# K's bias added on VectorE, the next sequence's transposes moved ahead, and a rearranged opening in a fused attention and mixing kernel

## The reference, cut to what matters

```python
h = layernorm(x) * (1 + ca) + sa
Q, K, V = h @ Wq + bq, h @ Wk + bk, h @ Wv + bv      # 16 heads of 8 channels
Q, K = elu(Q) + 1, elu(K) + 1
KV = einsum('nshd,nshm->nhmd', K, V);  Z = 1 / (einsum('nlhd,nhd->nlh', Q, K.sum(1)) + 1e-6)
h1 = layer_norm(h + (Q @ KV * Z) @ Wo + bo)          # g1, beta1
a  = layer_norm(h1 + relu(h1 @ W1 + b1) @ W2 + b2)   # g2, beta2
x  = x + ga * a
h2 = layernorm(x) * (1 + cb) + sb
x  = x + gb * sigmoid(mix_r(h2) @ W_r) * (relu(mix_k(h2) @ W_k)**2 @ W_v)
```

## Time and profile before

| what | value |
|---|---|
| median of 3 runs | 162.54 us (162.42 to 162.72) |
| the profiled execution, its own time | 162.81 us |
| its span in the trace | 160.7 us |
| PE busy | 155.6 us, 97% of the span |
| PEld busy | 145.1 us, 90% |
| VectorE busy | 123.1 us, 77% |
| ScalarE busy | 127.3 us, 79% |
| GpSimd busy | 104.6 us, 65% |
| TensorE clock granted | 9 tenths or more in all 40 slices |

### The profile page before, as it was taken

How to read it: one execution, slowest core, us unless ns; L and a number is a source line. 1 busy time by engine, 2 the same in 40 slices (tenths; PEclk the granted TensorE clock), 3 DMA queues, 4 the chain that set the end, 5 groups by cost and what they waited for, 6 DMA issues and landing times.

```text
span 160.7 us, 4111 instructions
## 1 busy us (share of the span) xinstructions
PE 155.6 (97%) x1151; PEld 145.1 (90%) x1151; DVE 123.1 (77%) x572; ACT 127.3 (79%) x346; POOL 104.6 (65%) x243
## 2 busy tenths in 40 slices
PE   7899999999999999999999999999999999999992
PEld 6778998999999999999999999999999999888891
DVE  3766878597887969696978779796969777888842
ACT  4256777889797979898997979797989989656562
POOL 4337567576676767787676767676877755973631
PEclk9999999999999999999999999999999999999999
DMA  4926299920010101010100101010101001010112
GB/s 122 269 90 174 67 276 369 423 115 0 2 37 0 33 0 33 4 37 0 34 5 0 33 4 35 0 35 4 33 0 35 4 0 33 2 37 0 35 33 67
DMA packets 8974, 9.94 MB, mean 62 GB/s; under 512 B 724, under 2 KB 7416, under 8 KB 8952
## 3 DMA queue, kind: packets, MB, share of 16 engines
q1 hardware_dynamic: 8656, 9.60, 18.8%
q10 hardware_dynamic: 296, 0.08, 0.2%
HBM read 7.55 MB, written 2.13 MB: 60 GB/s over the span
## 4 chain that ended last, share of the span: by engine, by line
PE 93%; DMA 2%; DVE 2%; ACT 1%; issue 0%; SPq 0%; DVEq 0%
PE bank L1266 16%; PE bank L1156 16%; PE bank L1145 8%; PE bank L1238 5%; PE bank L1194 5%; PE bank L1150 5%; PE bank L1222 4%; PE bank L1182 4%; PE bank L1230 4%; PE bank L1378 4%; PE bank L1210 4%; PE bank L1206 4%; PE bank L1249 3%; DMA kqvo<-in_kqvo 2%; PE bank L1219 1%; PE bank L1398 1%
## 5 line engine op out<-in xcount | busy, mean ns | idle before, releaser
L1156 PE MATMUL bank<-w,hid 128*128 128x128 f32 x240 | 31.7, 275 | 0.0
L1266 PE MATMUL bank<-x1T,w 128*128 128x256 f32 x120 | 30.9, 381 | 0.0
L1156 PEld LDWEIGHTS bank<-w,hid 128*128 128x128 f32 x240 | 29.3, 192 | 0.0
L347 ACT ACTIVATE hid<-bank,b_cols 128x256 f32<-128x256 f32 x60 | 26.0, 511 | 1.1 <-PE bank L1266 1.1
L544 POOL TENSOR_TENSOR rstd_n<-vare_n,power 128x2 f32<-128x2 f32 x30 | 23.8, 792 | 2.4
L1266 PEld LDWEIGHTS bank<-x1T,w 128*128 128x128 f32 x120 | 21.5, 190 | 2.7 <-DVE z L803 0.2
L710 DVE TENSOR_SCALAR ny<-bank,mv_ny,rstd_ny 128x128 f32<-128x128 f32 x32 | 11.7, 406 | 9.0 <-POOL rstd_ny L544 9.0
L323 ACT ACTIVATE hT<-bank,modT 128x256 f32<-128x256 f32 x16 | 9.0, 565 | 11.3 <-PE bank L1145 11.3
L540 POOL TENSOR_TENSOR vare_n<-mv_n,eps 128x2 f32<-128x2 f32 x30 | 5.9, 195 | 17.2 <-DVE mv_n L704 17.1
L292 ACT ACTIVATE n<-x_all,shift_n,rstd_n 128x128 f32<-128x128 f32 x27 | 11.8, 485 | 2.5 <-POOL shift_n L552 2.5
L317 ACT ACTIVATE keepT<-bank,modT 128x255 f32<-128x255 f32 x26 | 13.1, 555 | 0.0
(11 more groups left out here) (187 smaller groups left out, 454.7 us busy)
## 6 DMA issues: line engine op xcount, KB each, us to landing
gm_rows<-mod_rows_dram SPq DMA_DIRECT2D x2, 960.0 KB, 9.5
out<-out_sb SPq DMA_DIRECT2D x15, 128.0 KB, 1.8
gm_rows<-mod_rows_dram SPq DMA_DIRECT2D x1, 768.0 KB, 6.7
w<-in_w SPq DMA_DIRECT2D x1, 512.0 KB, 5.6
x_all<-in_x SPq DMA_DIRECT2D x1, 512.0 KB, 5.6
bv_row<-bv_rows_dram SPq DMA_DIRECT2D x1, 512.0 KB, 7.1
bv_row<-bv_rows_dram SPq DMA_DIRECT2D x1, 384.0 KB, 4.4
gm_rows<-mod_rows_dram SPq DMA_DIRECT2D x1, 384.0 KB, 3.7
```

The source lines that it names most:

```text
L347: last = nc.scalar.activation(hid[:, f, :], bank[:, f % 2 * L:(f % 2 + 1) * L], ACT.Relu, bias=b1_cols[:, f:f + 1])
L1156: last = nc.tensor.matmul(banks[6][:, c * D:(c + 1) * D], hid[:, f, c * 128:(c + 1) * 128], w2[:, f, :], start=False, stop=(f == FF - 1 an ...
L1266: return nc.tensor.matmul(bank[:, f % 2 * L:(f % 2 + 1) * L], w1[:, f * 128:(f + 1) * 128], x1T[:, :], start=True, stop=True)
```

## The change

1. K's bias. The bf16 product in front of Wk's products goes, with the instructions that split the bias in two. Now `bias_rows` holds the bias in all 128 rows, and VectorE adds it, bank 4 plus `bias_rows` into the new SBUF tile `kb` (`k_biased`); `k_exponent` and `k_elu` read `kb`. Sequence 0 alone still gets its bias on TensorE, as a float32 product.
2. In a step, `n1_transposes` of the next sequence stand ahead of the last hidden tile's two products of `feed_forward_out` (the last two pairs of records), no longer at the start of the next step. The statistics of x are taken two sequences ahead, late in VectorE's step; `rstd` and `shift` of n1 have two buffers.
3. VectorE's order in a step: the gate (`gated`) ahead of z's statistics, `centred` ahead of the denominators, the two `mix_half`s apart.
4. The opening: sequence 0 is turned from a plain normalised copy; `bv_product` is made once, and `direct_row` copies its row by a product with `ident`; ScalarE takes `k_exponent(2)` after `x1_turned(0)`; VectorE takes `x_stats(4)` and `x_mv(4)` at the end of the opening.

```diff
             def k_exponent(s):
-                need(act, k_mm, s + 1)
-                nc.scalar.activation(exp_k[:, :, :], chunked(banks[4]), ACT.Exp, bias=neg1[:, :]).then_inc(expk_ok, 1)
+                if s == 0:
+                    act.wait_ge(k_mm, 1)
+                need(act, kb_ok, s)
+                source = kb[:, :, :] if s else chunked(banks[4])
+                nc.scalar.activation(exp_k[:, :, :], source, ACT.Exp, bias=neg1[:, :]).then_inc(expk_ok, 1)
...
-                k_exponent(2)
                 q_exponent(2)
+                q_relu()
                 attention_turned(1)
                 x1_turned(0)
-                q_relu()
+                k_exponent(2)
...
-            bias_part(0)
-            n1_chunk(0, 1).then_inc(n1_half, 1)
+            normalise("n1", n1[1], x_chunk(0), 1, n1_turn)
...
+            def k_biased(s):
+                need(dve, k_mm, s + 1)
+                need(dve, bias_rows_ok, 1)
+                nc.vector.tensor_tensor(kb[:, :, :], chunked(banks[4]), bias_rows[:, :].unsqueeze(1).broadcast_to([128, NC, D]),
+                                        ALU.add).then_inc(kb_ok, 1)
...
                 k_elu(2)
+                q_elu(2)
                 x_stats(3)
                 x_mv(3)
                 y_stats(1)
                 norm_mv("ny", 2)
-                q_elu(2)
                 second_columns()
                 shift_columns()
                 y_norm(1)
                 masked_state(2)
+                x_stats(4)
+                x_mv(4)
...
+                if live(t):
+                    centred(sp_)
+                    denominators(sb_)
+                    reciprocals(sb_)
+                    k_biased(sa)
+                    attention(sb_)
+                    if live(t - 4):
+                        mix_half(K_W, sc)
+                    k_elu(sa)
...
             def direct_row(s):
...
-                nc.tensor.matmul(dest, modT[:, ROW, s:s + 1].broadcast_to([128, 128]), wv, start=True, stop=False)
-                nc.tensor.matmul(dest, part128[:, :], bv_pad[:, :], start=False, stop=True).then_inc(direct_mm, 1)
+                pe.wait_ge(bv_ok, 1)
+                nc.tensor.matmul(banks[2][:, s * D:(s + 1) * D], ident[0:S, s:s + 1].broadcast_to([S, 128]), bv_rows[:, :],
+                                 start=True, stop=True).then_inc(direct_mm, 1)
...
             def k_product(s):
...
-                nc.tensor.matmul(chunked(banks[4]), ones3[:, :], bias_parts[:, :].unsqueeze(1).broadcast_to([128, NC, D]),
-                                 start=True, stop=False)
...
+                feed_forward_out(2, 3)
+                if live(t + 1):
+                    n1_transposes(sa + 1)
+                feed_forward_out(3, FF).then_inc(z_mm, 1)
```

More of the change, by code:

```diff
@@ L76, in build @@
         bv_rows = sb("bv_rows", [S, D])
-        bias3 = sb("bias3", [3, D])
-        bias_k = sb("bias_k", [3, D])
-        part_mask = sb("part_mask", [3, 2])
-        high = [sb(f"high{i}", [3, D], BF16) for i in range(2)]
-        rest = sb("rest", [3, D])
-        bias_parts = sb("bias_parts", [128, D], BF16)
+        bias_rows, bv_bias = sb("bias_rows", [128, D]), sb("bv_bias", [S, D])
         x_all = sb("x_all", [128, S * NC, D])
@@ L290, in take_n1 @@
                 wait_x(act, s)
-                for c in chunks:
-                    last = nc.scalar.activation(n1[s % 2][:, c, :], x_all[:, NC * s + c, :], ACT.Identity,
-                                                scale=rstd["n1"][:, c:c + 1], bias=shift_n1[:, c:c + 1])
+                for c in range(NC):
+                    last = n1_part(s, c)
                 last.then_inc(n1_ok, 1)
-            take_n1(0, (0,))
+            act.wait_ge(bias_mm, 1)
+            act.wait_ge(const_pool, 1)
+            nc.scalar.activation(bias_rows[:, :], banks[6][:, D:2 * D], ACT.Identity, scale=-1.0,
+                                 bias=one_pair[:, 0:1]).then_inc(bias_rows_ok, 1)
+            act.wait_ge(x_in[0], 16)
+            act.wait_ge(shift_n1_ok, 1)
+            n1_part(0, 0)
             act.wait_ge(cols_ok, 2)
@@ L942, in step @@
                 step_end(t - 1)
-                y_first = t == S
-                if live(t + 1):
-                    x_stats(t + 1)
-                    need(dve, stats_ok["n1"], sa + 2)
+                if live(t):
[4 more added lines that the diff above has]
+                    attention(sb_)
+                    if live(t - 4):
+                        mix_half(K_W, sc)
+                    k_elu(sa)
+                    middle(sp_)
+                    need(dve, x2_ok, sp_ + 1)
+                    norm_stats("n3", lambda c: x2_p[:, c, :])
+                    if live(t - 4):
+                        mix_half(R_W, sc)
+                    norm_mv("n3", sp_ + 1)
+                    y_stats(sb_)
+                    q_elu(sa)
+                    norm_mv("ny", sb_ + 1)
+                    if live(t + 2):
+                        x_stats(t + 2)
+                        x_mv(t + 2)
+                    masked_state(sa)
+                    shift_of_n3(sp_)
+                    y_norm(sb_)
+                    return
@@ L963, in step @@
-                if live(t):
-                    k_elu(sa)
                 middle(sp_)
-                if y_first:
-                    y_stats(sb_)
-                    norm_mv("ny", sb_ + 1)
+                y_stats(sb_)
+                norm_mv("ny", sb_ + 1)
                 need(dve, x2_ok, sp_ + 1)
                 norm_stats("n3", lambda c: x2_p[:, c, :])
-                if live(t - 4) and not draining(t):
-                    mix_half(K_W, sc)
-                    mix_half(R_W, sc)
                 norm_mv("n3", sp_ + 1)
-                if not y_first:
-                    y_stats(sb_)
@@ L977, in step @@
-                if live(t):
-                    q_elu(sa)
-                if not y_first:
-                    norm_mv("ny", sb_ + 1)
-                if t == S:
-                    y_norm(sb_)
-                    gated(sc)
-                if live(t):
-                    masked_state(sa)
-                    shift_of_n3(sp_)
-                else:
-                    take_n3(t)
-                if not y_first:
-                    y_norm(sb_)
+                y_norm(sb_)
+                gated(sc)
@@ L1386, in step, with value_of_mix @@
                     feed_forward_out(3, FF).then_inc(z_mm, 1)
-                else:
-                    feed_forward_out(2, FF).then_inc(z_mm, 1)
+                    return
+                if t == 3:
+                    feed_forward_out(0, 2)
+                    value_of_state(sa)
+                    need(pe, hidb_ok, sd + 1)
+                else:
+                    value_of_state(sa)
+                    feed_forward_out(0, 2)
+                if live(t - 4):
+                    value_of_mix(sc)
+                feed_forward_out(2, 3)
+                if live(t + 1):
+                    n1_transposes(sa + 1)
+                feed_forward_out(3, FF).then_inc(z_mm, 1)
+            def value_of_mix(s):
+                need(pe, ksq_ok, s + 1)
+                need(pe, wvg_ok, s + 1)
+                need(pe, q_ok, s + 5)
+                need(pe, prod_ok, s)
+                for c in range(NC):
+                    last = nc.tensor.matmul(banks[5][:, c * D:(c + 1) * D], ksqT[:, c * 128:(c + 1) * 128], gate_tile(s)[:, :],
+                                            start=True, stop=True)
+                last.then_inc(v_mm, 1)
             steps(step)
```

209 lines of the change are left out of this document (94 added, 115 removed).

## The result

The changed kernel takes 165.91 us (165.88 to 166.08), the kernel before 162.63 us (162.42 to 163.94) in the same comparison. The ratio is 1.0189, interval 1.0163 to 1.0216: slower by 1.9%. In the traces the span goes from 160.7 to 164.2 us, 3.5 more. The prediction named +2.1.

A forecast was written before the change was run, and what follows sets the result against it. The prediction took the step as bound twice, by TensorE's sum and ScalarE's chain to y. The opening's +0.9 and the steady steps' +1.2 gave +2.1: profiled 162.81 to 164.9, median 162.54 to 164.6, range 162.0 to 165.8.

The forecast's parts named there:

- the likeliest case: Whole kernel: both the opening and the steady step lose time; 164.6 us, own range 163.7 to 165.5, chance 0.52.
- the fifth case: Steady step: the state product is late too and kb near 0.5; 0.2 or more a step, 165.7 to 166.5, chance 0.08.
- Bound twice: Steady step: TensorE's sum and ScalarE's chain to y take equally long, both setting the 8.78 us step.
- The meeting of 62.91 and 62.96: Step 7 before the change: attT ends at 62.91, y's first weight load starts at 62.96, so ScalarE lets y start.
- The bias product is worth nothing while the chain stays: Steady step: removing the bias product's 0.11 from TensorE gains nothing as long as ScalarE's chain to y stays.
- y at 4.42 from z's end, step 8.89: Steady step: y starts 4.42 behind z's last product instead of 4.31, making the step 8.89 instead of 8.78.
- The terms of the 0.11: Steady step's loss: 0.06 for exp_k's wait for kb plus 0.05 for reading SBUF.
- k_elu: VectorE's steady step: starts at 3.10, ends at 3.51; the state product wants it at about 3.55 to 3.65.
- Eleven steps: Steps 5 to 15: 11 steps each lose 0.11, together +1.2 us (0 to 2.2).
- The opening, +0.9: Opening through step 4: exp_k(2) behind x1T(0) delays k_elu(2) and z(0)'s statistics; y of step 4 moves by +0.9.
- The gain of 0.6 at `k_elu(0)`: Opening: earlier transposes of sequence 0 and fewer small products bring 0.6 at k_elu(0), about 0.4 left at x1T(0).
- The rival on the other side, TensorE as the bound,: Steps 3 to 15: TensorE alone sets the step, -1.4, and -0.4 from the opening; 160.7 us, chance 0.11.

The follow-up runs named there:

- e3: The kernel before the change, with ScalarE's attT copy ahead of the first hid copy in each step: 163.30 us, ratio 1.0026.
- e2: The changed kernel with ScalarE's attT copy ahead of the first hid copy in each step: 162.68 us, ratio 0.9967 to the kernel before.
- e8: The changed kernel with n1_transposes back at the start of the next step: 164.36 us, ratio 1.0081 to the kernel before.
- e12: The changed kernel with centred behind the reciprocals instead of ahead of the denominators: 164.30 us, ratio 1.0086 to the kernel before.
- e7: The changed kernel with exp_k still waiting for kb but reading bank 4 in PSUM: 165.36 us, ratio 1.0149 to the kernel before.
- e1: The changed kernel with GpSimd's plus_row(2) ahead of first_scale(3) and norm_scale(ny, 2) in the opening: 165.66 us, ratio 1.0141 to the kernel before.
- e4: The changed kernel with K's bias back on TensorE as a bf16 product for sequences 1 to 15, without kb: 163.89 us, ratio 1.0042 to the kernel before.
- e9: The changed kernel with attT ahead of the first hid copy, plus_row(2) first, x_stats(3) and x_mv(3) ahead of k_elu(2): 160.90 us, ratio 0.9869.
- e10: The kernel of e9 with K's bias back on TensorE as a bf16 product, without kb: 161.46 us, ratio 0.9906 to the kernel before.

## Why the prediction held, and where it was off

The direction and the mechanisms were right, and the likeliest case came about. Its sum of +2.1 was 1.0 short of the ratio's +3.1 (162.54 x 0.0189) and 1.4 short of the span's 3.5, so the time (165.6 by the ratio, 165.91 as measured) lies just above the 163.7 to 165.5 given for that case, where the fifth case (165.7 to 166.5) begins. That case's mechanism did not occur: `kb`'s addition is 0.36 long, and the state product starts 3.76 behind u's start, before 3.86.

- **Bound twice.** Right to within 0.05, and shown from both sides: e3 leaves 8.77, e2 gives 8.68 (forecast for TensorE alone 8.67). The meeting of 62.91 and 62.96 was that of the weight load, which starts 0.05 behind `attT`'s end as in the changed kernel (74.17 and 74.22). y's record came 0.05 behind its load before, and starts with it now. So TensorE's sum set y before, with 0.05 to spare on ScalarE's side.
- **The bias product is worth nothing while the chain stays.** No run takes it away and leaves all else. The nearest are e8 and e12, which have no bias product and no wait for `kb`: their step is 8.81, and without the 0.03 of `exp_k`'s source (e7) that is an estimated 8.78, as before. By the same estimate y starts about 0.05 sooner than before, and the time behind y grows by as much (next point).
- **y at 4.42 from z's end, step 8.89.** y came at exactly 4.42, the step at 8.93. The missing 0.04 lies behind y: from y to z's end 4.51, where the forecast had 8.78 - 4.31 = 4.47. In e2, where nobody waits, it is 4.46 (72.85 to 77.31). y's first record takes 0.16 to the next instead of 0.11 when it had to wait. The forecast moved y and left what follows as it was.
- **The terms of the 0.11.** `kb`'s start at 1.98 was 0.12 early (2.10), 0.09 of it `centred`, taken at the 0.43 that it had in another place of the queue; its 0.41 was 0.05 too long. The loss by the wait was 0.12, not 0.06, and the 0.05 for the source was 0.03 to 0.04. ScalarE's chain was otherwise 0.05 shorter, because y now starts 0.05 behind `attT`'s end, before 0.10. That y came at exactly 4.42 is partly luck: errors of both signs cancel.
- **k_elu.** Forecast to start at 3.10 and to end at 3.51; it starts at 72.96 - 69.80 = 3.16 and ends at 3.58. The state product's first weight load follows at 3.63, so there is nothing to spare, and y's delay covers it.
- **Eleven steps.** 11 x 0.15 = 1.6 instead of 1.2, and 0.2 for the stall, which the forecast did not have.
- **The opening, +0.9.** This is the term that was mis-sized: 1.64. The steps of the forecast up to `k_elu(2)` and `y_norm(1)` came 0.14 and 0.18 late. Then z(0)'s statistics came at 26.24 instead of 25.54, because z(0) ended at 26.04 and not, as the forecast had it, by about 24.8. I had followed VectorE's and ScalarE's queues past the late `k_elu(2)`, and not GpSimd's, in which `plus_row(2)` stands behind roots whose input is late because of it; TensorE waits 1.44 for its result. e1 shows this at 0.53: there z(0)'s statistics start at 25.74, 0.20 from the forecast. e4 shows that 0.8 of the opening's loss goes with `kb`, of which the forecast names only the wait of `exp_k(3)`.
- **The gain of 0.6 at `k_elu(0)`** was 0.43 (8.94 to 8.51), and `x1T(0)` came at 19.00, not 18.83. One trace of each can't tell this gain from the loading times: among the traces with the changed opening `exp_k(0)` alone varies by 0.58.
- **The rival on the other side, TensorE as the bound,** needed ScalarE's way from ny's transposes to y 0.11 shorter. It did not happen, but its condition was the right one: e2 shortens that way by 0.36, and the step is 8.68, although `kb` is ready only at 2.46 there too. The Trainium skill's rule to optimize the engine of the highest occupancy first (Perfetto Trace Analysis, section Identifying the Most-Contended Engine) is borne out once the swap is in (e9 against e10, 0.09 a step) and was wrong for the change alone; TensorE's busy shares in e9 and in the changed kernel differ by one point (97% and 96%).

What stays open: why the single 0.2 in step 5, and why e3's step 4 grew by 0.15.
